# One operand of VectorE's weighing and of the edge sort's marks is read from PSUM instead of SBUF, in a four-layer graph network on one core

## The chip, the cores and the metric

The kernel runs on one core of one Trainium2 chip. The metric is the device time of one execution in microseconds (us), here the median of three runs. Matrix work is TensorE's (PE in the profile), elementwise work VectorE's (DVE) and ScalarE's (ACT), indirect DMAs are issued by GpSimd (POOL), plain ones by SyncE (SP).

## The reference

A graph of 6250 nodes with 256 features and 106250 edges, already sorted by destination, goes through four layers. Each is followed by a residual and a layer norm.

```python
src, dst = edge_index                       # 106250 edges, sorted by dst
# layer 0 (GIN)
agg = segment_sum(x[src], dst);   out = relu(bn(relu(bn(((1+eps)*x + agg) @ W1)) @ W2 + x))
# layer 1 (attention over edges, 8 heads of 32)
sim = einsum('hed,hed->eh', q[dst], k[src]) * scale
p = exp(sim - segment_max(sim, dst)[dst]);  attn = p / segment_sum(p, dst)[dst]
agg = segment_sum(attn * v[src], dst)
# layer 2 (edge attributes summed by SOURCE node, plus degree and centrality terms)
sum3d = segment_sum(edge_attr @ W_sum, src)
# layer 3 (gated; mean of neighbours in both directions, then a GRU cell)
```

## The kernel before

The kernel is a chain of eleven stages with a barrier after each (`end_stage`). The nodes are cut into NW = 49 blocks of 128. The edges are cut into NC = 832 chunks of 128, and the work over edges is STEPS = 880 steps: a chunk that spans two blocks of nodes is taken once for each. U = 16 steps make an iteration, QUAD = 4 steps are handled by one VectorE instruction, HALF = 8 steps is the depth of the rings of one-hot matrices, OCT = 8 chunks go together where edge rows are sorted.

A segment sum is a matrix product: VectorE compares the destinations of a chunk with `iota_row` (`compare`, L195, four chunks in one instruction of 128x512 elements) and TensorE multiplies this one-hot matrix by the chunk's rows into the PSUM bank of the block. ScalarE copies a finished bank out and clears it (`take_banks`, L186 and L188).

Three stages matter here.

**The first gather** (`first_gather`) sums the rows of x over the incoming edges. GpSimd issues 832 indirect gathers (L578), four at a time, into a ring of 16 slots; before each four it waits for `s_used`, which SyncE passes on when TensorE has used the slots. TensorE runs 880 products (L612). Beside this, `bin_positions` works out where each edge goes when edges are sorted by source: it *counts* edges by block of source nodes in a first half and *ranks* them in a second. Each takes 104 instructions called `mark` (L472): 8 chunks of source blocks, compared with the numbers 0 to 48 from `iota_row`, which gives a bf16 one-hot of 128x392. In the second half `widen` (L480), `place` (L488 and L491) and TensorE's `rank` (L435, L437) follow each mark. The mark's PSUM neighbours are `bp_counts` (two banks) and `bp_spread` (two banks).

**The weighted sums** (`weighted_sums`) compute the sum of attn * v and the sum of attn per block. SyncE loads the gathered v rows in quads of 512 KB (L1473) into `ring`, 16 slots; from the fifth quad on it waits until the quad that lay there is weighed. VectorE handles each quad with three instructions: `hot` compares (L195) and copies the 8 attention weights per edge beside the row (L1514); `weigh` (L1524) multiplies 128x1024 elements of `ring` by the weights, which are read from `k.sims` and repeated 32 times:

```python
weight = k.sims[:, s * HEADS:(s + QUAD) * HEADS].rearrange("p (s h) -> p s h", h=HEADS)
dve.tensor_tensor(weighted[...], ring[...], weight.unsqueeze(3).to_broadcast([P, QUAD, HEADS, HD]), ALU.mult)
```

`weighted` and `onehot` hold 8 steps, so VectorE may be two quads ahead of TensorE's products (L1504). In the same stage the edge attributes are sorted by source: GpSimd scatters 568 chunks of edge rows (71 octs of 8, L1280) from the two buffers of `staging` to `bin_rows` in DRAM. SyncE loads an oct (520 KB, L1265) after every third quad (WS_PACE = 12), in the same queue, and first waits until the scatters of the oct two before have landed. So a period of the stage is one oct of scatters on GpSimd, and on SyncE one load of an oct and three loads of quads, which stand behind it in order.

**The edge scores** (`edge_scores`) and the **last gathers** (`last_gathers`) are not touched. They also have GpSimd issue an indirect DMA per chunk (L1166, L2083) beside VectorE, and are read for comparison. In the edge scores VectorE multiplies a query row in PSUM by a key row in SBUF (L1239).

The order of work on each engine is the order in the code. Semaphore waits are the only coupling.

## Time and profile before

| what | value |
|---|---|
| three runs | 7632.49, 7638.13, 7615.44 us |
| median | 7632.49 us |
| span of the profiled execution, first to last instruction | 7527.2 us |
| the profiled execution's own time | not among the figures at hand; the span lies 105.3 us under the median of the runs |
| busy: PE, DVE, ACT, POOL | 5373.7, 3160.7, 545.2, 4732.4 us |
| mean granted TensorE clock | 0.750 of full speed |
| first gather | about 58 to 1360 us of the span |
| weighted sums | about 3400 to 4276 us of the span |

The busy times are sums over stages with different limits, so a change in a stage has to be read from the rows of that stage. "Idle before" is the time for which the engine did nothing before the instructions of a group, and the names behind it say what ended it.

### The profile page before, as it was taken

The page shows a single profiled execution, that of the slowest core. Times are in us where ns is not written, and L with a number is a line of the kernel's source. Part 1 is how long each engine was busy: PE and PEld are TensorE (multiplying, and loading weights), DVE is VectorE, ACT ScalarE, POOL GpSimd, SP SyncE. Part 2 cuts the span into 40 slices and gives each one's busy share as a digit, 9 for nine tenths or more (in the row PEclk, how much of TensorE's full clock was granted, in tenths as well). Part 3 has the DMA queues.
Part 4 walks back from the last instruction along what each step waited for, and adds up shares of the span by engine and source line. Part 5 has one row for each costly group of instructions (what it writes and reads, how often), then busy time and mean ns, then how long its engine had stood idle before and what let it go on. Part 6 is the DMA issues. An engine that isn't in the chain of part 4 may idle for free. (4 is left out here: it accounts for less than half of the span.)

```text
span 7527.2 us, 81611 instructions
## 1 busy us (share of the span) xinstructions
PE 5373.7 (71%) x17807; PEld 3065.0 (41%) x17807; DVE 3160.7 (42%) x6956; ACT 545.2 (7%) x1542; POOL 4732.4 (63%) x4778
## 2 busy tenths in 40 slices
PE   5666777638765556636566687788888888888887
PEld 2333333525332223324444575433433344444444
DVE  2222444528655556674444567511111123333317
ACT  0000000324000000010000001100000000000004
POOL 5666665664666666677677404766666666666665
PEclk8777777969767777767778899865555588888869
DMA  4444433331688888846667675433333333333445
GB/s 137 133 134 130 124 123 121 128 100 66 214 256 256 265 262 268 266 134 210 210 217 226 205 191 148 126 89 89 90 89 87 89 111 119 119 119 119 123 101 191
DMA packets 693161, 1164.20 MB, mean 155 GB/s; under 512 B 104128, under 2 KB 490285, under 8 KB 692614
## 3 DMA queue, kind: packets, MB, share of 16 engines
q0 software_dynamic: 224288, 633.55, 28.9%
q1 hardware_dynamic: 468344, 525.21, 21.9%
q8 instruction: 217, 3.56, 0.2%
q14 instruction: 202, 1.65, 0.1%
q10 hardware_dynamic: 110, 0.23, 0.0%
HBM read 870.83 MB, written 287.77 MB: 154 GB/s over the span
## 5 line engine op out<-in xcount | busy, mean ns | idle before, releaser
L2126 PE MATMUL l_sums<-big 128*128 (+1 forms) x3520 | 1701.9, 578 | 349.1 <-issue 135.1
L195 DVE TENSOR_TENSOR big<-iota_row,dst_tab 128x512 f32<-128x512 f32 x660 | 458.4, 695 | 2171.3 <-PE l_sums L2126 712.1
L1280 POOL DMA_INDIRECT bin_rows<-staging,place_tab x832 | 979.6, 1177 | 337.4 <-issue 249.1
L1166 POOL DMA_INDIRECT big<-kv_rows,idx_tab x880 | 832.0, 945 | 503.0 <-issue 241.1
L578 POOL DMA_INDIRECT big<-in_x,big x832 | 826.6, 994 | 483.6 <-SPq L148 237.7
L2083 POOL DMA_INDIRECT big<-x_rows,place_tab x880 | 882.3, 1003 | 394.9 <-issue 241.7
L2083 POOL DMA_INDIRECT big<-x_rows,idx_tab x832 | 817.2, 982 | 426.7 <-issue 226.6
L1220 PE MATMUL es_q<-big 128*128 x1760 | 720.9, 536 | 450.3 <-issue 343.3
L2126 PEld LDWEIGHTS l_sums<-big 128*128 128x128 f32 x3520 | 765.2, 259 | 502.0 <-issue 473.7
L612 PE MATMUL l_sums<-big 128*128 x1760 | 723.0, 543 | 331.9 <-issue 235.8
L1504 PE MATMUL ws_sums<-big 128*128 128x264 f32 x1760 | 546.1, 474 | 321.2 <-DVE big L1524 170.9
L1220 PEld LDWEIGHTS es_q<-big 128*128 128x128 f32 x1760 | 380.6, 252 | 747.7 <-issue 714.1
L612 PEld LDWEIGHTS l_sums<-big 128*128 128x128 f32 x1760 | 393.8, 255 | 623.9 <-issue 587.7
L1239 DVE TENSOR_TENSOR big<-es_q,big 128x256 f32<-128x256 f32 x880 | 370.8, 423 | 547.4 <-remote 274.3
L1504 PEld LDWEIGHTS ws_sums<-big 128*128 128x128 f32 x1760 | 400.6, 236 | 467.7 <-issue 384.9
L178 PEld LDWEIGHTS l_spare<-ones 128*1 128x1 bf16 x1760 | 139.7, 79 | 906.7 <-issue 906.7
L1244 DVE TENSOR_REDUCE sims<-big 128x8 f32<-128x256 f32 x880 | 356.1, 410 | 0.0
L1524 DVE TENSOR_TENSOR big<-big,sims 128x1024 f32<-128x1024 f32 x220 | 268.7, 1221 | 180.5 <-DMA big<-v_edge 173.6
L195 DVE TENSOR_TENSOR big<-iota_row,bin_tab 128x512 f32<-128x512 f32 x220 | 151.8, 692 | 440.4 <-PE l_sums L2126 263.8
L178 PE MATMUL l_spare<-ones 128*1 128x1 bf16 x1760 | 289.3, 164 | 3.4 <-issue 3.4
L1581 PE MATMUL as_sums<-sims 128*128 128x129 f32 x1760 | 249.8, 298 | 56.2 <-DVE sims L195 54.9
L1581 PEld LDWEIGHTS as_sums<-sims 128*128 128x128 f32 x1760 | 232.8, 189 | 74.5 <-issue 67.9
(297 smaller groups left out, 5187.4 us busy)
## 6 DMA issues: line engine op xcount, KB each, us to landing
v_edge<-big SPq DMA_DIRECT2D x880, 128.0 KB
big<-v_edge SPq DMA_DIRECT2D x220, 512.0 KB
bin_rows<-big SPq DMA_DIRECT2D x110, 520.0 KB
sims<-bin_rows SPq DMA_DIRECT2D x110, 520.0 KB
staging<-in_edges SPq DMA_DIRECT2D x104, 520.0 KB
gate_rows<-big SPq DMA_DIRECT2D x49, 512.0 KB
big<-gate_rows SPq DMA_DIRECT2D x49, 512.0 KB
big<-kv_rows,idx_tab POOLq DMA_INDIRECT x880
```

The costliest lines, as they stand in the source:

```text
L178: pe.matmul(spare, ones[:, 0:1], ones[:, 0:1], start=True, stop=True)
L195: return dve.tensor_tensor(out, rows, columns.unsqueeze(2).to_broadcast([P, QUAD, P]), ALU.is_equal)
L578: pool.indirect_dma_start(ring[:, u, 0:D], None, table, bass.IndirectOffsetOnAxis(ap=k.by_chunk[:, c:c + 1], axis=0)).then_inc(s_row[u], 16)
L612: pe.matmul(sums[:, bank_of(node[u], width)], onehot[:, u % HALF, :], flat[:, bass.ds(slot_of(s, node[u], D + 1), width)], start=False, st ...
L1166: pool.indirect_dma_start(ring[:, u, :], None, k.kv_rows, bass.IndirectOffsetOnAxis(ap=k.idx[:, s:s + 1], axis=0)).then_inc(s_row[u], 16)
L1220: pe.matmul(qps[u % 4][:, 0:D], onehot[:, u % HALF, :], query[:, bass.ds(block_at[u] * D, D)], start=True, stop=True).then_inc(s_q, 1)
L1239: dve.tensor_tensor(prod[:, u % 2, :], qps[u % 4][:, 0:D], ring[:, u, 0:D], ALU.mult).then_inc(s_prod, 1)
L1280: pool.indirect_dma_start(k.bin_rows, bass.IndirectOffsetOnAxis(ap=k.place[:, c:c + 1], axis=0), k.staging[:, g % 2, j, :], None).then_inc ...
L1504: pe.matmul(sums[:, bank_of(node[s % U], AW)], onehot[:, s % HALF, :], weighted[:, s % HALF, :], start=False, stop=True, skip_group_check= ...
L1581: pe.matmul(sums[:, bank_of(node[s % U], EW)], onehot[:, s % U, :], ring[:, q % RING, r, 2:2 + EW], start=False, stop=True, skip_group_che ...
L2083: pool.indirect_dma_start(ring[:, u, :], None, k.x3_rows, bass.IndirectOffsetOnAxis(ap=column, axis=0)).then_inc(s_row[u], 16)
L2126: pe.matmul(sums[:, bank_of(node[u] + turn, D)], onehot[:, u % HALF, :], flat[:, bass.ds(at, D)], start=False, stop=True, skip_group_check ...
```

## The change

In the weighted sums two PSUM tiles `ws_side0` and `ws_side1` of 128x128 are added (the stage then uses six banks). Once per iteration of 16 steps VectorE copies the iteration's 128 weights from `k.sims` to one of them (`keep`, 55 copies of 128x128), an iteration ahead, and both `hot`'s small copy and `weigh` read the weights from there. In `bin_positions` VectorE copies the numbers 0 to 48 once for each of the two halves to an unused part of a PSUM bank that is not written in that half (`bp_spread0` while counting, `bp_counts` while ranking), and all marks read them from there.

```diff
@@ bin_positions
+    numbers = spread[0][:, OCT * NW:OCT * NW + NW], counts[:, 1, ROWS // 2:ROWS // 2 + NW]
...
         def mark(n, g):
 
             if g == 0:
-                dve.wait_ge(s_row, 2)
+                if n:
+                    dve.wait_ge(s_wins, 3)
+                else:
+                    dve.wait_ge(s_row, 2)
+                dve.tensor_copy(numbers[n], k.iota_row[:, 0:NW]).then_inc(s_number, 1)
+                dve.wait_ge(s_number, n + 1)
...
-            dve.tensor_tensor(hot[:, g % 2, :, :], k.iota_row[:, 0:NW].unsqueeze(1).to_broadcast([P, OCT, NW]),
+            dve.tensor_tensor(hot[:, g % 2, :, :], numbers[n].unsqueeze(1).to_broadcast([P, OCT, NW]),
                               bin_f[:, g * OCT:(g + 1) * OCT].unsqueeze(2).to_broadcast([P, OCT, NW]),
                               ALU.is_equal).then_inc(s_hot, 1)
@@ weighted_sums
+        side = [psum(nc, ctx, f"ws_side{i}", [P, U * HEADS]) for i in range(2)]
...
+            def weights(s):
+
+                at = s % U * HEADS
+                return side[s // U % 2][:, at:at + QUAD * HEADS].rearrange("p (s h) -> p s h", h=HEADS)
+
+            def keep(it):
+
+                if it >= 2:
+                    dve.wait_ge(s_weight, (it - 1) * U)
+                    dve.wait_ge(s_side, (it - 1) * U)
+                dve.tensor_copy(side[it % 2][:, :], k.sims[:, it * U * HEADS:(it + 1) * U * HEADS]).then_inc(s_kept, 1)
...
-                dve.tensor_scalar(weighted[:, s % HALF:s % HALF + QUAD, D:], k.sims[:, s * HEADS:(s + QUAD) * HEADS].rearrange(
-                    "p (s h) -> p s h", h=HEADS), 1.0, None, ALU.mult).then_inc(s_side, QUAD)
+                dve.wait_ge(s_kept, s // U + 1)
+                dve.tensor_scalar(weighted[:, s % HALF:s % HALF + QUAD, D:], weights(s), 1.0, None,
+                                  ALU.mult).then_inc(s_side, QUAD)
...
-                weight = k.sims[:, s * HEADS:(s + QUAD) * HEADS].rearrange("p (s h) -> p s h", h=HEADS)
+                weight = weights(s)
...
+            keep(0)
             for s in range(0, STEPS, QUAD):
+                if s % U == 0 and s + U < STEPS:
+                    keep(s // U + 1)
                 hot(s)
                 weigh(s)
```

VectorE's instructions at the start of the weighted sums, before (`big` holds `ring`, `weighted` and `onehot`):

```order
L1528 MEMSET big 1x512
L195 TENSOR_TENSOR big<-iota_row,dst_tab 128x512
L1514 TENSOR_SCALAR big<-sims 128x4x8
L1524 TENSOR_TENSOR big<-big,sims 128x4x256
L195 TENSOR_TENSOR big<-iota_row,dst_tab 128x512
L1514 TENSOR_SCALAR big<-sims 128x4x8
L1524 TENSOR_TENSOR big<-big,sims 128x4x256
```

And with the change:

```order
L1548 MEMSET big 1x512
L1526 COPY ws_side<-sims 128x128 x2
L195 TENSOR_TENSOR big<-iota_row,dst_tab 128x512
L1534 TENSOR_SCALAR big<-ws_side 128x4x8
L1544 TENSOR_TENSOR big<-big,ws_side 128x4x256
L195 TENSOR_TENSOR big<-iota_row,dst_tab 128x512
L1534 TENSOR_SCALAR big<-ws_side 128x4x8
L1544 TENSOR_TENSOR big<-big,ws_side 128x4x256
```

Nothing is reordered; a copy comes in ahead of every fourth quad, two ahead of the first. L1524 becomes L1544, and L1514 becomes L1534.

VectorE at the start of the ranking half in the first gather, with the change:

```order
L195 TENSOR_TENSOR big<-iota_row,dst_tab 128x512 x2
L469 COPY bp_counts<-iota_row 128x49
L478 TENSOR_TENSOR big<-bp_counts,sims 128x392
L486 TENSOR_TENSOR big<-ident,sims 49x392
L195 TENSOR_TENSOR big<-iota_row,dst_tab 128x512
L478 TENSOR_TENSOR big<-bp_counts,sims 128x392
L486 TENSOR_TENSOR big<-ident,sims 49x392
```

The mark, L472 before, is L478 now, and one copy stands ahead of the first. The widening (L480, now L486) still reads both operands from SBUF. The other engines' instructions are the same as before.

## Rows read from the trace of the kernel before

**Rows 1.** Groups of instructions by line in the weighted sums, 3400 to 4276 us.
```profile
line engine op names shapes xcount | busy us, mean ns | idle before us <-releasers
L1280 POOL DMA_INDIRECT bin_rows<-staging,place_tab x568 | 637.4, 1122 | 239.7 <-issue 184.9 <-DMA staging<-in_edges 39.0 <-POOLq L108 15.8
L1504 PE MATMUL ws_sums<-big 128*128 128x264 f32 x1760 | 546.1, 474 | 321.2 <-DVE big L1524 170.9 <-issue 149.0 <-ACT ws_sums L188 1.0
L1524 DVE TENSOR_TENSOR big<-big,sims 128x1024 f32<-128x1024 f32 x220 | 268.7, 1221 | 180.5 <-DMA big<-v_edge 173.6 <-remote 3.7 <-PE ws_sums L1504 2.5
L195 DVE TENSOR_TENSOR big<-iota_row,dst_tab 128x512 f32<-128x512 f32 x220 | 153.3, 697 | 266.2 <-PE ws_sums L1504 160.4 <-remote 78.3 <-issue 27.5
L1514 DVE TENSOR_SCALAR big<-sims 128x32 f32<-128x32 f32 x220 | 51.0, 232 | 0.0
```
**Rows 2.** Waits of SyncE's queue and of GpSimd there: total us, times, longest.
```profile
SPq L1265 <- DMA bin_rows<-staging,place_tab: 200.4, 21, 11.7
SPq L1473 <- DVE big L1524: 117.4, 53, 14.4
...
POOL bin_rows L1280 <- DMA staging<-in_edges: 39.0, 4, 12.8
```
**Rows 3.** The scatters of that stretch alone: min/median/max ns, first and last start.
```profile
L1280 POOL DMA_INDIRECT bin_rows<-staging,place_tab x568: 963/969/2033, 3400.3 to 4260.6; - x190
```
**Rows 4.** Timeline of one period: start, length in us, engine, line, [idle before].
```profile
3547.96 1.23 DVE L1524 TENSOR_TENSOR big<-big,sims 128x1024 f32<-128x1024 f32 x1 [4.48 <-DMA big<-v_edge]
3548.51 1.52 POOL L1280 DMA_INDIRECT bin_rows<-staging,place_tab  x1 [0.30 <-issue]
...
3552.16 0.97 POOL L1280 DMA_INDIRECT bin_rows<-staging,place_tab  x1 [0.30 <-issue]
3553.20 0.35 SPq L1265 DMA_DIRECT2D staging<-in_edges  x1
...
3553.59 1.56 SPq L1473 DMA_DIRECT2D big<-v_edge  x3
...
3561.37 0.69 DVE L195 TENSOR_TENSOR big<-iota_row,dst_tab 128x512 f32<-128x512 f32 x1 [0.95 <-remote]
3561.61 1.29 POOL L1280 DMA_INDIRECT bin_rows<-staging,place_tab  x1 [0.30 <-issue]
```
**Rows 5.** Edge scores: GpSimd's gathers, and VectorE's product that reads PSUM; min/median/max ns.
```profile
L1166 POOL DMA_INDIRECT big<-kv_rows,idx_tab x880: 940/946/1002, 1942.0 to 3260.8; - x176
...
L1239 DVE TENSOR_TENSOR big<-es_q,big x880: 412/425/426, 1946.0 to 3277.0; 128x256 f32<-128x256 f32 x176
```
**Rows 6.** Last gathers, first half: GpSimd's gathers twice, then VectorE's compares, 4800 to 6037 us.
```profile
L2083 POOL DMA_INDIRECT big<-x_rows,idx_tab x832: 940/946/1461, 4803.5 to 6036.2; - x167
...
L2083 POOL DMA_INDIRECT big<-x_rows,idx_tab x832 | 817.2, 982 | 426.7 <-issue 226.6 <-SPq L148 189.8 <-POOLq L108 10.3
...
L195 DVE TENSOR_TENSOR big<-iota_row,dst_tab 128x512 f32<-128x512 f32 x219 | 151.7, 693 | 1027.1 <-PE l_sums L2126 712.1 <-issue 191.1 <-remote 123.8
```
**Rows 7.** First gather: gathers twice, the mark, the widening, and the place's product that reads PSUM.
```profile
L578 POOL DMA_INDIRECT big<-in_x,big x832: 940/946/1656, 58.7 to 1351.6; - x167
...
L578 POOL DMA_INDIRECT big<-in_x,big x832 | 826.6, 994 | 483.6 <-SPq L148 237.7 <-issue 229.5 <-POOLq L108 16.4
...
L472 DVE TENSOR_TENSOR big<-iota_row,sims 128x392 bf16<-128x392 f32 x208 | 116.5, 560 | 0.0
...
L480 DVE TENSOR_TENSOR big<-ident,sims 49x392 f32<-49x392 f32 x104 | 57.7, 555 | 0.0
L488 DVE TENSOR_TENSOR big<-bp_spread,big 128x392 f32<-128x392 f32 x104 | 57.5, 553 | 0.0
```
**Rows 8.** Busy time and DMA in the 8 us behind a load of an oct, and in the 3 us after.
```profile
core 0: us, PE busy (x) PEld busy (x) DVE busy (x) ACT busy (x) POOL busy (x), PEclk, DMA share, GB/s
3553.00:3561.00 8.00, 4.83 (x18) 3.41 (x18) 3.94 (x6) 0.00 (x0) 6.17 (x7) 0.93 0.91 284
3561.00:3564.00 3.00, 3.00 (x8) 2.28 (x8) 1.91 (x3) 0.00 (x0) 2.39 (x3) 0.50 0.37 122
```
**Rows 9.** Timeline of a stall in the weighted sums.
```profile
3655.36 0.69 DVE L195 TENSOR_TENSOR big<-iota_row,dst_tab 128x512 f32<-128x512 f32 x1 [12.83 <-remote]
...
3657.70 0.51 SPq L1265 DMA_DIRECT2D staging<-in_edges  x1
...
3662.76 1.53 POOL L1280 DMA_INDIRECT bin_rows<-staging,place_tab  x1 [10.43 <-DMA staging<-in_edges]
```
**Rows 10.** A VectorE pass over 128x128 elements between PSUM and SBUF, in the softmax stage.
```profile
L1395 DVE TENSOR_SCALAR big<-sm_t 128x128 f32<-128x128 f32 x55 | 11.8, 288 | 3.2 <-PE sm_t L1362 2.7 <-issue 0.4
```

More of the change, by code:

```diff
@@ L387, in bin_positions @@
     spread = [psum(nc, ctx, f"bp_spread{i}", [P, 512]) for i in range(2)]
-    s_fill, s_filled, s_key, s_hot, s_counted, s_line, s_start, s_wins, s_spread, s_taken, s_row, s_wide = sems(
+    numbers = spread[0][:, OCT * NW:OCT * NW + NW], counts[:, 1, ROWS // 2:ROWS // 2 + NW]
+    s_fill, s_filled, s_key, s_hot, s_counted, s_line, s_start, s_wins, s_spread, s_taken, s_row, s_wide, s_number = sems(
         nc, k, *(f"bp_{n}" for n in ("fill", "filled", "key", "hot", "counted", "line", "start", "wins", "spread",
-                                     "taken", "row", "wide")))
+                                     "taken", "row", "wide", "number")))
     COUNT_AT, LINE_AT, PLACE_AT = 4, 424, 452
@@ L1460, in weighted_sums @@
         sums = psum(nc, ctx, "ws_sums", [P, BANKS * BANK])
-        s_zeros, s_hot, s_weight, s_side, s_sum, s_taken, s_free = sems(
-            nc, k, *(f"ws_{n}" for n in ("zeros", "hot", "weight", "side", "sum", "taken", "free")))
+        side = [psum(nc, ctx, f"ws_side{i}", [P, U * HEADS]) for i in range(2)]
+        s_zeros, s_hot, s_weight, s_side, s_sum, s_taken, s_free, s_kept = sems(
+            nc, k, *(f"ws_{n}" for n in ("zeros", "hot", "weight", "side", "sum", "taken", "free", "kept")))
         s_v = sems(nc, k, *(f"ws_v{q}" for q in range(U // 2)))
```

## The prediction

> **What bounds the kernel now.** The change touches two of eleven stages, so I read those, and two others for comparison. In the weighted sums the groups by line come first [rows 1]. VectorE is busy for 268.7 + 153.3 + 51.0 = 473 of 876 us and TensorE for 546.1; both wait for a large part. GpSimd hardly does. Its 568 scatters take 637.4 us, and of its 239.7 us idle 184.9 lie between one scatter and the next without any wait (0.33 us each), 15.8 at the start; only 39.0 us are a wait, for the load of an oct. 637.4 + 184.9 + 39.0 + 15.8 = 877.1: the whole stage. SyncE confirms it: it stood 200.4 us until scatters had landed before it could load the next oct [rows 2], and the loads of v stand behind that load in its queue, so VectorE's wait for v (173.6 us) and TensorE's for VectorE (170.9 us) are made there. GpSimd's scatters pace this stage.
>
> Then the length of a scatter. Its median is 969 ns, its least 963 and its most 2033 [rows 3], the mean 1122. The timeline shows what lengthens it [rows 4]: a scatter that starts during L1524 takes 1.52 us and ends at 3550.03, 0.84 us after L1524 (3549.19); one with VectorE quiet takes 0.97 us. The same under the compare L195: 1.29 us, end at 3562.90, 0.84 us after L195 (3562.06). So GpSimd comes soon after its start to a point that it can't pass while VectorE runs one of these two, and both read two operands from SBUF. The control is the edge scores: there 880 products L1239 read one operand from PSUM, and of 880 gathers none took over 1002 ns against a median of 946 [rows 5].
>
> **The weighing.** Scatters above their median: 568 x (1122 - 969) ns = 87 us. This is due to L1524 and L195, and the change takes only L1524 out of it. What L195 alone costs I take from the last gathers, where nearly all that VectorE does is L195: 832 x (982 - 946) ns = 30 us for 219 of them [rows 6]. The weighted sums have 220, and gathers there are spaced alike, so 30 us remain. It may be less, since a scatter held by L1524 today can't be held by the L195 behind it; then what is left is today's share of L195. Term: -(87 - 30) = **-57 us**. Bounds: -87 if nothing holds a scatter, and 0 if a PSUM operand does not free it. I take -57 because the rows 5 and 6 show both halves of it at hundreds of instructions.
>
> Can the rest of the stage follow? A period (an oct of scatters, three quads) lasts 877 / 71 = 12.4 us now and would last 8 x (0.969 + 30/568 + 0.326) = 10.8 us, without the waits. VectorE's work in a period is 3 x (1.22 + 0.70 + 0.23) = 6.5 us, TensorE's 546.1 / 73 = 7.5 us. DMA: after a load of an oct is issued the engines are 0.91 busy for 8 us and then 0.37 [rows 8], so a burst of 2.1 MB needs some 8 of the 10.8 us. All three fit.
>
> In four places the period was not GpSimd's: VectorE stood for up to 12.83 us for something that the profile puts down as "remote", the loads in SyncE's queue came late, and GpSimd then waited, once 10.43 us [rows 9], in sum 39.0 us in four waits [rows 2]. I see no wait in the code for it, and leave it as it is. But a shorter period leaves less in hand when it happens: about 1 us more in each of the four waits, **+4 us**.
>
> **What the weighing costs.** L1544 has as many elements as L1524. A PSUM operand does not change the pace: L488 with one takes 553 ns, L480 of as many elements per partition, all in SBUF, 555 [rows 7]. The 55 copies into PSUM I take at the 288 ns of a 128x128 pass out of PSUM [rows 10]: 16 us of VectorE. Each follows a wait for VectorE's own last instruction, some 0.1 us. What hides them is VectorE's idle time, 180.5 + 266.2 us in the stage; without it they would be 16 to 22 us on the path. Their operand in SBUF is one, so by rows 5 they hold no scatter; if they did, 16 us of cover against 473 would add 2 us. **0 us**, at most +2.
>
> **The marks.** In the first gather the gathers lie 832 x (994 - 946) ns = 40 us above their median [rows 7]. L195's part is 30 us again; 10 are left for 208 marks and 104 widenings, which keep both operands in SBUF and will, in the second half, catch some gathers that the mark before them holds now. So 7 to 10 us of GpSimd's time go. But GpSimd is not alone on the path: it waited 237.7 us for slots that TensorE had not yet used [rows 7], and where such a wait follows, a shorter gather only lengthens the wait. Half counts: **-4 us**, between 0 and -10. Two copies of 128x49 are nothing.
>
> **Sum.** -57 + 4 - 4 = -57 us. The profiled execution's own time is not shown; its span of 7527.2 us goes to 7470, and what lies around it I leave alone: 7632.5 - 57 = **7576 us** against the median, -0.7%.
>
> **Rivals.**
> *The hold does not depend on where the second operand lies.* Then nothing moves but 20 us of hidden copies: 7632 us. Against it stand 880 gathers beside L1239; for it only that L1239 is shorter (0.42 us), which would make holds shorter, not absent. Chance 0.04. The Trainium skill has a rule on this side: "SBUF — State Buffer", section "Who interferes with whom", says that a VectorE instruction with two SBUF inputs stands in the way of a GpSimd instruction that reads SBUF, not of one that only writes it, and infers that generating a DMA's descriptors needs only the write side, so that `tensor_tensor` does not delay it. By that, today's scatters would not be held and the change would be worth 0; the trace of rows 3, 4 and 6 disagrees, at least for indirect DMAs.
>
> *The stalls take it back.* The bursts of loads follow each other at 10.8 us with 8 us of DMA work, so a late burst runs into the next, SyncE's queue stands, and GpSimd waits more often. Each stall as in rows 9 costs about 10 us; if their number doubles, 39 us come back: -57 + 39 = -18, 7615 us. From about three more on the gain is under 0.3%. For it: four stalls exist. Against: most periods today end with the DMA engines at 0.37. Chance 0.11.
>
> *VectorE becomes the bound,* because the weights in PSUM, repeated 32 times and read beside TensorE's writes to other banks, come slowly. Place: L1544. Its three per period fit until 3 x (0.93 + w) = 10.8, w = 2.7 us; from w = 3.2 us on the stage is slower than today. At 3.5 us, 73 x 3 x 4.43 = 970 us against 876: about 7722 us. Against it: L488 reads PSUM beside TensorE's products at the pace of L480 [rows 7], and the 880 of L1239 never took over 426 ns [rows 5]. Chance 0.03.
>
> *More is saved:* L195's share stays at what it is today, and the stalls shrink with luck: 57 becomes 72 to 87, 7545 to 7560 us. Chance 0.12, faster too.
>
> **How the numbers follow.** The forecast, -35 to -72 us, has 0.70. About 0.3% (23 us) is what a measurement of this kernel can tell from no change. Faster: 0.70 + 0.12 and the part of the stalls that leaves over 23 us (0.03), 0.85. Same: 0.04 + 0.07, 0.11. Slower: 0.03 and 0.01 for stalls beyond that, 0.04. The range runs from 7547, nearly the lower bound of GpSimd's share, to 7615, where the stalls have doubled.
>
> **What would show it.** L1280 in the weighted sums: mean from 1122 to about 1022 ns, busy 580 us, and no scatter that ends 0.84 us after L1544. L1544 at 1.22 us; L1526 at 0.2 to 0.3. The stage from 876 to about 824 us. L578's mean from 994 to about 985. L1166 and L2083 as before. I am wrong if L1280's mean stays above 1080 (the hold), if it falls and GpSimd's wait for `staging` grows by as much (stalls), or if L1544 passes 2 us.

## The result and the profile after

The changed kernel took **7708.1 us** (median of four runs, 7674.6 to 7719.8) against 7624.0 us (7597.0 to 7638.1, four runs) for the kernel before: ratio 1.0104, 95% interval 1.0074 to 1.0134. It is 1% slower. The forecast was 7576, 0.7% faster, and the range ended at 7615.

The profiled execution has a span of 7697.6 us. By stage, before and after: first gather 1307 and 1302 us, edge scores 1337 and 1383, weighted sums **876 and 978**, last gathers 2525 and 2554. Edge scores and last gathers have the same instructions in both kernels; in the other profiles they lie between 1323 and 1384 and between 2510 and 2560 us (the last comparison below apart), so their part of the difference is not the change's. Nor is all of the 170 us between the two spans: the execution profiled before (7527.2 us) was about 100 us shorter than the runs beside it. The comparison of `ws_only` with `marks_only` below, which stand side by side on one chip, is the cleaner one: stages of 960 and 875 us, kernels of 7607.3 and 7511.7.

The groups by line of the weighted sums in the changed kernel, which answer to [rows 1]:

```profile
line engine op names shapes xcount | busy us, mean ns | idle before us <-releasers
L1286 POOL DMA_INDIRECT bin_rows<-staging,place_tab x568 | 571.4, 1006 | 398.4 <-DMA staging<-in_edges 200.4 <-issue 182.2 <-POOLq L108 15.9
L1511 PE MATMUL ws_sums<-big 128*128 128x264 f32 x1760 | 548.3, 471 | 420.4 <-issue 210.3 <-DVE big L1544 206.0 <-ACT ws_sums L188 3.4
L1544 DVE TENSOR_TENSOR big<-big,ws_side 128x1024 f32<-128x1024 f32 x220 | 266.2, 1210 | 10.7 <-issue 5.4 <-DMA big<-v_edge 5.3
L195 DVE TENSOR_TENSOR big<-iota_row,dst_tab 128x512 f32<-128x512 f32 x220 | 152.5, 693 | 526.0 <-remote 327.8 <-PE ws_sums L1511 139.5 <-issue 57.6
...
L1526 DVE COPY ws_side<-sims 128x128 f32<-128x128 f32 x55 | 16.1, 294 | 1.8
```

The scatters did what was forecast and more: mean 1122 to 1006 ns, 637.4 to 571.4 us. But GpSimd's wait for its edge rows in `staging` went from 39.0 us in 4 waits [rows 2] to 200.4. VectorE no longer waits for v (173.6 to 5.3 us) but in front of the compare L195, 266.2 to 526.0 us, most of it "remote". The same in the waits of the stage:

```profile
SPq L1480 <- DVE big L1544: 418.3, 112, 19.2
SPq L1271 <- DMA bin_rows<-staging,place_tab: 28.9, 5, 9.0
...
POOL bin_rows L1286 <- DMA staging<-in_edges: 200.4, 20, 14.8
```

SyncE used to wait for scatters to land (200.4 us, now 28.9) and now waits for VectorE (117.4, now 418.3). The pace has passed from GpSimd to VectorE, which is busy for only 435 of 978 us. Its timeline (start, length, [idle before]) shows the form of the loss, the one of [rows 9]:

```profile
4106.54 0.69 DVE L195 TENSOR_TENSOR big<-iota_row,dst_tab 128x512 f32<-128x512 f32 x1 [13.29 <-issue]
4107.15 0.18 DVE L1534 TENSOR_SCALAR big<-ws_side 128x32 f32<-128x32 f32 x1
4107.26 1.21 DVE L1544 TENSOR_TENSOR big<-big,ws_side 128x1024 f32<-128x1024 f32 x1
4117.12 0.69 DVE L195 TENSOR_TENSOR big<-iota_row,dst_tab 128x512 f32<-128x512 f32 x1 [8.65 <-remote]
```

L195 waits for one thing, `s_sum`, TensorE's count of its products. From the trace's records of that semaphore, beside the ends of the products (counted from 0; the ends are modelled):

```
4090.33 product 571 ends   (the one that L195 of 4106.54 needs)
4096.93 product 575 ends   (the one that L195 of 4117.12 needs)
count +1 at 4095.14 4099.40 4102.93 4112.05 4115.55
count +1 at 4116.98 4117.02 4117.07 4117.11 4117.15 4117.19
```

One count has no record: the one that lets L195 go, whose wait ends at 4106.5. Counts come 3 to 6 us apart, where products 572 to 575 end 0.8 to 0.9 us apart; then six come within 0.21 us, quicker than TensorE makes products (two matmuls of 0.47 us each). So products had been done that were not yet counted: **the counts are late, not the products**. L195 of 4106.54 starts 16 us after the modelled end of the product that it needs. I measured for each compare how long after both (VectorE free, product ended) it starts. Sum of those over 1 us late, and number over 5 us: before 132 us and 9, after 453 us and 37.

It is TensorE's counts that are late. VectorE's own are on time in the same stage: of the 219 quads behind the first, none has its first product over 0.56 us after L1544 has ended and TensorE is free, and SyncE, when it waits for VectorE, issues the load of v 0.03 us after L1544. ScalarE, which waits for TensorE's counts too, starts up to 12.1 us after the last product that ended.

The records have gaps of their own. In the weighted sums 682 of TensorE's 881 counts have one, and 121 of VectorE's 220 weighings; in the kernel before it is 644 and 138, in `after_busy` and in the last comparison below all of them. In `before_deep` records are missing (703 of 881) and no compare is late, so a missing record alone makes no late count. Whether the capture of the profile has a part in the delay is open: no run here was timed without a span captured on its core.

On the product ends the Trainium skill ("Perfetto Trace Analysis", section "Tensor Engine Instruction (MATMUL, LD_WEIGHTS)") says that the profiler estimates them, and that the count is sent only when PSUM has acknowledged the write and has then to propagate. So an ending in the profile is not a count; the bursts are what tells late counts from slow products here.

While this stall lasts GpSimd scatters on at its full pace, until `staging` is empty (SyncE's next load stands behind the v loads, which stand behind VectorE):

```profile
4108.38 0.97 POOL L1286 DMA_INDIRECT bin_rows<-staging,place_tab  x1 [0.30 <-issue]
...
4112.20 0.97 POOL L1286 DMA_INDIRECT bin_rows<-staging,place_tab  x1 [0.30 <-issue]
4124.34 0.97 POOL L1286 DMA_INDIRECT bin_rows<-staging,place_tab  x1 [11.17 <-DMA staging<-in_edges]
```

The burst of counts comes at 4117, 3.8 us after the last scatter ended at 4113.2. All the stalls that end in a burst (three counts or more, each at most 0.08 us behind the other: 22 after, 5 before; one more comes behind the very last scatter) end in a pause of GpSimd, 1.3 to 4.8 us after it ran dry. This gives the **theory**: a stream of scatters without breaks delays TensorE's counts to VectorE; the change makes the stream denser. **Rivals**: something that the change adds (the PSUM reads, the copies, their waits); nothing following the products on TensorE; the number of counts; VectorE's short lead of two quads.

### The profile page after: what moved, and what is told of

It is laid out like the page before. It is cut to its first block and busy times, and to the rows that moved or that the text cites. A ratio compares the mean times of both kernels' runs of the same rounds, so it can differ in the third digit from the quotient of the medians.

```text
span 7697.6 us, 81941 instructions
## 1 busy us (share of the span) xinstructions
PE 5365.1 (70%) x17807; PEld 3045.6 (40%) x17807; DVE 3167.0 (41%) x7013; ACT 545.2 (7%) x1542; POOL 4658.5 (61%) x4778
## 5 line engine op out<-in xcount | busy, mean ns | idle before, releaser
L2149 PE MATMUL l_sums<-big 128*128 (+1 forms) x3520 | 1681.4, 571 | 398.8 <-issue 154.0
L195 DVE TENSOR_TENSOR big<-iota_row,dst_tab 128x512 f32<-128x512 f32 x660 | 457.7, 694 | 2452.4 <-PE l_sums L2149 742.8
L1286 POOL DMA_INDIRECT bin_rows<-staging,place_tab x832 | 913.4, 1098 | 490.2 <-issue 246.6
L2106 POOL DMA_INDIRECT big<-x_rows,place_tab x880 | 885.2, 1006 | 397.7 <-issue 238.3
L584 POOL DMA_INDIRECT big<-in_x,big x832 | 818.1, 983 | 484.8 <-SPq L148 236.5
L178 PEld LDWEIGHTS l_spare<-ones 128*1 128x1 bf16 x1760 | 139.2, 79 | 892.8 <-issue 892.8
L195 DVE TENSOR_TENSOR big<-iota_row,bin_tab 128x512 f32<-128x512 f32 x220 | 151.7, 691 | 441.9 <-PE l_sums L2149 274.6
L178 PE MATMUL l_spare<-ones 128*1 128x1 bf16 x1760 | 288.8, 164 | 1.0 <-issue 1.0
L1544 DVE TENSOR_TENSOR big<-big,ws_side 128x1024 f32<-128x1024 f32 x220 | 266.2, 1210 | 10.7 <-issue 5.4
L2062 PE MATMUL gp_g<-sims,big 128*128 128x512 f32 x392 | 237.5, 690 | 40.2 <-DVE big L2022 35.7
```

Of the source, the lines that this page charges most:

```text
L178: pe.matmul(spare, ones[:, 0:1], ones[:, 0:1], start=True, stop=True)
L195: return dve.tensor_tensor(out, rows, columns.unsqueeze(2).to_broadcast([P, QUAD, P]), ALU.is_equal)
L584: pool.indirect_dma_start(ring[:, u, 0:D], None, table, bass.IndirectOffsetOnAxis(ap=k.by_chunk[:, c:c + 1], axis=0)).then_inc(s_row[u], 16)
L1286: pool.indirect_dma_start(k.bin_rows, bass.IndirectOffsetOnAxis(ap=k.place[:, c:c + 1], axis=0), k.staging[:, g % 2, j, :], None).then_inc ...
L2106: pool.indirect_dma_start(ring[:, u, :], None, k.x3_rows, bass.IndirectOffsetOnAxis(ap=column, axis=0)).then_inc(s_row[u], 16)
L2149: pe.matmul(sums[:, bank_of(node[u] + turn, D)], onehot[:, u % HALF, :], flat[:, bass.ds(at, D)], start=False, stop=True, skip_group_check ...
```

## The experiments

Each comparison has its own runs of the kernel before beside it, on the same chip, and ratios are to those. Stage times are the weighted sums in the profile; "late" is the sum and number defined above.

### Which part of the change

`ws_only` is the change in `weighted_sums` alone, `marks_only` that in `bin_positions` alone. `copies_only` keeps the 55 copies into PSUM and VectorE's wait for them, but reads the weights from SBUF:

```diff
-                at = s % U * HEADS
-                return side[s // U % 2][:, at:at + QUAD * HEADS].rearrange("p (s h) -> p s h", h=HEADS)
+                return k.sims[:, s * HEADS:(s + QUAD) * HEADS].rearrange("p (s h) -> p s h", h=HEADS)
```

Expected of `ws_only`:

> The change in the weighted sums alone; the marks read SBUF as before. In the profile of the changed kernel the weighted sums took 968 us between the first and last product against 867, the first gather 1288 against 1292. Theory 1 (late counts: the loss is in the weighted sums, where VectorE waits in front of L195 for TensorE's count of products while TensorE has nothing to do): all of the loss stays, about 7700 us, and the scatters' mean near 1006 ns with GpSimd's wait for staging near 200 us. Rival (the marks, or code that is displaced, cost the time in other stages): near 7625 us.

Expected of `marks_only`:

> The marks alone read PSUM; the weighted sums are those of before. Theory 1: 7620 us, the gathers' mean in the first gather near 983 ns against 994, the stage shorter by 4 to 8 us, the weighted sums near 870 us with GpSimd's wait for staging near 40. Rival (displaced code makes the stalls): weighted sums well above 900 us here too.

Expected of `copies_only`:

> The changed kernel with its copies of the weights into PSUM and its waits, but both reads of the weights go back to SBUF, so that L1524's hold on GpSimd is there again; the marks stay in PSUM. Theory 2 (VectorE's hold was a break in GpSimd's stream of scatters, and without breaks TensorE's counts reach VectorE late): the stage comes back to 870 to 890 us, waits in front of L195 as 'remote' to about 90 us, the ratio to the kernel before 0.997 to 1.002. Rival (the added copies and waits disturb VectorE): the stage stays near 960 us, ratio 1.012.

Measured: `ws_only` 1.0119 [1.0088, 1.0150], stage 960 us, late 419 us. `marks_only` 0.9987 [0.9965, 1.0010], stage 875. `copies_only` 1.0019 [0.9994, 1.0043], stage 875, scatters 1141 ns, late 138 us. The loss is the weighted sums', and there not the copies' or the waits': it comes with the PSUM operand of L1544, that is with what this does to the scatters, or with the PSUM reads themselves.

### What TensorE does behind a product, and how often it counts

```diff
                 pe.matmul(sums[...], onehot[...], weighted[...], ...).then_inc(s_sum, 1)
+                push(pe, k, spare[:, 0:1])
```

is `after_push` and `before_push`: a 1x1 product (L178) behind each product, as the gather stages have it. `after_quad_count` lets TensorE count by 4 on the last product of a quad, a quarter of the counts.

Expected of `after_push`:

> The changed kernel, with a product of one column by one (L178, the helper push that the last gathers have) behind every product of the weighted sums. Theory 1 (a finished product is counted late while nothing follows it on TensorE): the counts come in time, VectorE's 328 us of waiting as 'remote' in front of L195 go, GpSimd's wait for staging falls from 200 us to under 40, the stage takes 800 to 830 us and the kernel about 7560 to 7590. Rival (VectorE's wait comes of its own added copies and waits, or of its instruction supply): no change but 880 small products, 7700 us or a little more.

Expected of `before_push`:

> The kernel before with the same small product behind every product of the weighted sums. Theory 1: the four stalls of 39 us in all go, the scatters' mean stays near 1122 ns, the stage 830 to 850 us, the kernel 7590 to 7610. Rival: 7625 us or a little more.

Expected of `after_quad_count`:

> The changed kernel, but TensorE counts its products four at a time, on the last of each quad, instead of one by one. Theory 2 with a backlog of counts as its core: a fourth of the counts makes a backlog shorter, GpSimd's wait for staging falls from 190 us to under 60, the stage takes 810 to 850 us, ratio 0.985 to 0.995, faster than both. Rival (the products themselves are late, not their counts): 960 us as before, ratio 1.012.

Measured: `after_push` 1.0140 [1.0103, 1.0176], stage 948, late 256 us with up to 24.7 in one compare, GpSimd's wait for staging 150.7; `before_push` 1.0097 [1.0067, 1.0127], stage 947, late 147 us. Neither forecast came true: something that follows at once does not end the stalls. The smaller sum after the change is no cure, since VectorE now waits longer for the products themselves (279.5 us in place of 139.5; in the kernel before 319.9 in place of 160.4, where the stage loses 71 us).

`after_quad_count` 1.0107 [1.0080, 1.0135], stage 985, GpSimd's wait for staging 208.8 us, late 467 us: as the change. I had forecast a gain, and by the expectation this outcome speaks for slow products; the bursts above speak against those. What it does rule out is the number of counts. The Trainium skill ("TensorE: Matmul & The Clock Gate", section "The cost: per-tile semaphore tail") prices a count at some 26 ns and advises one on the last product. Here a quarter of the counts gave nothing, and delays of 10 us are hundreds of times that price.

### With no scatters, and with breaks between them

`after_no_scatter` leaves out the loads and scatters of edge rows in the weighted sums, but for the first two octs (the edge attributes are partly not sorted). `after_pause` puts a memset of 128x384 elements and a wait for it behind every fourth scatter:

```diff
-                spread_oct(pool, k, g)
+                for first in range(0, OCT, QUAD):
+                    spread_part(pool, k, g, first, QUAD)
+                    pool.memset(scratch, 0.0).then_inc(s_pause, 1)
+                    pool.wait_ge(s_pause, (g - EARLY_OCTS) * 2 + first // QUAD + 1)
```

`after_lumped` has nearly as many (140 for 142), four in a row after every second oct.

Expected of `after_no_scatter`:

> The changed kernel without the scatters of edge rows in the weighted sums but for the first two octs, and without the loads that feed them, so the edge attributes of layer 2 are partly left out. Theory 2: without GpSimd's stream no count is late; VectorE's waits in front of L195 as 'remote' vanish (under 20 us), the stage is bound by products and loads: 220 quads at 2.1 to 2.6 us, 460 to 570 us. Rival (the loads of v or the PSUM reads delay the counts): late counts of over 100 us remain.

Expected of `after_pause`:

> The changed kernel, but GpSimd makes a break after every fourth scatter: a memset of 128x384 of a scratch area and a wait for it, estimated at 0.5 to 0.8 us from the 0.20 us of a 128x128 memset, so about as much in all (142 breaks) as the holds took away. Theory 2: with the breaks the late counts go back to the level of before, GpSimd's wait for staging falls from about 190 us to 40 to 80, the stage takes 870 to 900 us although GpSimd has more to do, ratio near 1.00. Rival (reading the weights from PSUM beside TensorE's writes delays the products' counts): 960 to 1000 us, since GpSimd's breaks only add.

Expected of `after_lumped`:

> The changed kernel with the same GpSimd pauses as the kernel with a pause after every fourth scatter (142 memsets of 0.44 us with a wait behind each), but four of them one behind the other after every second oct, so that 16 scatters follow each other without a break and then comes one break of some 3 us. If what restores the time is that GpSimd's stream has breaks often, long counts come back: the stage is well above the 902 us of the kernel with the spread pauses, 930 to 980. If it is only GpSimd's pace, or the total time without scatters, the stage is about 902 us, ratio within 0.3% of 1.

Measured: without scatters (one execution) the stage takes 498 us, with the same products, v loads and PSUM reads, and late is 6 us in two compares. They are the control within the run: the 16 scatters that are left end at 3462.6 us, the two late compares start at 3457.2 (1.1 us late) and 3464.3 (5.2), and in the 470 us after them none is late. So neither the PSUM reads nor the v loads delay the counts. With pauses (`after_pause`): 0.9995 [0.9969, 1.0020], stage 902, just above the 870 to 900 expected, GpSimd's wait for staging 58.8 us. `after_lumped` 0.9988 [0.9965, 1.0012], stage 870:

```profile
L1286 POOL DMA_INDIRECT bin_rows<-staging,place_tab x568 | 573.9, 1010 | 215.8 <-issue 175.5 <-DMA staging<-in_edges 18.3 <-POOLq L108 15.8
...
L195 DVE TENSOR_TENSOR big<-iota_row,dst_tab 128x512 f32<-128x512 f32 x220 | 153.2, 697 | 389.9 <-PE ws_sums L1518 183.8 <-remote 183.0 <-issue 22.6
...
L1499 POOL MEMSET big<- 128x384 f32 x140 | 59.2, 423 | 6.1
```

Giving back to GpSimd the 65 us (59.2 + 6.1) that the change had taken from it takes GpSimd's wait from 200.4 to 18.3 us. I had expected breaks far apart to be worse than frequent ones (930 to 980 us if frequency mattered). They were not: four memsets, some 2 us, after every second oct are enough. The lateness fell less than the wait (298 us and 28 over 5 us, none over 11.1): a stall that ends before GpSimd runs dry does not cost GpSimd, which paces the stage, anything.

### Still denser, and a deeper ring

`after_no_hold` lets the compare read its row of numbers from PSUM too, so that nothing holds a scatter:

```diff
+        numbers = psum(nc, ctx, "ws_numbers", [P, P])
...
-                compare(dve, k, onehot[:, s % HALF:s % HALF + QUAD, :], None, k.dst[:, s:s + QUAD]).then_inc(s_hot, QUAD)
...
+                compare(dve, k, onehot[:, s % HALF:s % HALF + QUAD, :], numbers[:, :].unsqueeze(1).to_broadcast([P, QUAD, P]), k.dst[:, s:s + QUAD]).then_inc(s_hot, QUAD)
```

`after_deep` and `before_deep` make the rings `weighted` and `onehot` 16 steps deep (`DEEP = 2 * HALF`), so that VectorE may be four quads ahead.

Expected of `after_no_hold`:

> The changed kernel, with the numbers that the compare of the weighted sums takes read from a PSUM tile as well, so that no VectorE operation over many elements reads two operands from SBUF in that stage. Both theories: no scatter is held any more, mean from 1006 to about 970 ns, another 20 us of GpSimd's time gone (568 x 36 ns). The theory of late counts (the products' counts reach VectorE late for as long as GpSimd's scatters follow each other closely): the scatters leave still less room, so the stalls in front of the compare stay or grow, GpSimd waits 200 us or more for staging, and the stage takes 977 to 1000 us; ratio 1.010 or more. The rival (the time was lost to something that belongs to the weighing reading PSUM beside an operation with two operands in SBUF, or to the holds that are left): the stage takes less than with the change, 950 us or below.

Expected of `after_deep`:

> The changed kernel with rings of 16 steps in place of 8 for the weighed rows and for the rows of ones, so that VectorE may be four quads ahead of TensorE's counted products in place of two. If counts only arrive late (TensorE itself works on), eight products more of slack, some 3 to 5 us, absorb most stalls of 5 us and part of those of 10 to 18: GpSimd's wait for staging falls from 200 to below 80 us, the stage to 830 to 880 us, and the kernel is as fast as before or up to 0.6% faster. If TensorE's products themselves are slow, a deeper ring fills as well and nothing is gained: the stage stays at 960 us or more, ratio 1.010.

Expected of `before_deep`:

> The kernel before with the same rings of 16 steps, as the measure of what the rings alone bring: it had stalls too, 39 us of GpSimd's waiting for staging. If late counts are what the ring absorbs, the stage falls from 876 to 850 to 865 us and the ratio is 0.997 to 0.999, so the changed kernel with deep rings beats it by the rest of the holds removed (20 to 50 us). If nothing is absorbed: 876 us, ratio 1.

Measured: `after_no_hold` 1.0170 [1.0117, 1.0223], the slowest of the complete kernels, stage 1016 us:

```profile
L1286 POOL DMA_INDIRECT bin_rows<-staging,place_tab x568 | 551.6, 971 | 450.8 <-DMA staging<-in_edges 255.9 <-issue 179.1 <-POOLq L108 15.8
...
L195 DVE TENSOR_TENSOR big<-ws_numbers,dst_tab 128x512 f32<-128x512 f32 x220 | 151.7, 690 | 570.8 <-remote 383.0 <-PE ws_sums L1512 142.9 <-issue 44.1
```

Its longest scatter takes 982 ns. Twenty more us taken from GpSimd cost 38 us more of the stage; that is the theory's side, and the stage is longer than the 977 to 1000 us expected. The two ratios come from different comparisons, and their intervals touch.

The deep rings I had wrong. `after_deep` is at 1.0113 [1.0061, 1.0165], stage 953, late 479 us with up to 19.8: a lead of eight more steps absorbs nothing. That fell on the side that I had given to slow products. But the bursts are there, and the finding above explains it otherwise: a stall lasts until GpSimd stops, so a longer lead only moves the moment at which VectorE runs dry. Its bursts agree: most hold 11 to 15 counts, where the change has 4 to 6, and come 2.1 to 5.5 us after GpSimd ran dry. `before_deep` is at 1.0001 [0.9978, 1.0024], stage 867, with not one compare late, and its row shows why:

```profile
L1280 POOL DMA_INDIRECT bin_rows<-staging,place_tab x568 | 673.6, 1186 | 200.3 <-issue 184.7 <-POOLq L108 15.7
```

With VectorE never waiting for counts more scatters are held, and the mean is 1186 ns. Nor does the deep ring hide late counts here: among the records there is no burst. GpSimd did not wait for staging at all, yet the kernel is as fast as before: what stalls had cost (39.0 us), holds cost now (673.6 - 637.4 = 36 us). In the order of the scatter's mean length, the sums late of all kernels so far without added pauses: 1186 ns 0 us, 1141 ns 138, 1136 ns 103, 1122 ns 132, 1103 ns 147, 1049 ns 256, 1007 ns 419, 1006 ns 453, 998 ns 467, 992 ns 479, 971 ns 491. These come from several chips, one execution each. Part of this order could run the other way, since a VectorE that stands holds no scatter; in `after_no_hold` the length is set by the edit alone.

### What it is in the scatters

`after_busy` puts a memset of 128x1152 and a wait in the place of each scatter (the edge attributes are partly not written); `after_half_rows` cuts each scatter to its first 64 rows (the others are not written). Each ran once.

Expected of `after_busy`:

> The changed kernel with a GpSimd memset of about 1.2 us and a wait for it in the place of each of the 568 scatters of the weighted sums (the edge attributes are therefore partly not written); the loads of the octs stay and wait for the memsets. If a busy GpSimd is what delays TensorE's counts, there are waits of the compare of over 5 us as in the changed kernel and the stage is above 900 us. If it is the descriptors or their transfers, there are none: the compare's waits marked remote are below 30 us and the stage follows GpSimd at about 71 x 8 x 1.33 = 755 us, or whatever TensorE and VectorE need beyond that, up to 800 us.

Expected of `after_half_rows`:

> The changed kernel with every scatter of the weighted sums cut to the first 64 of its 128 rows (the edge attributes of the others are not written). If it is the number of descriptors, or of the small transfers, that crowds out TensorE's counts, half of them ends the stalls: compare's waits marked remote from 328 to below 100 us, GpSimd's wait for staging below 50 us. If it is the scatter instructions as such, whatever their size, the stalls stay or, where the scatters become shorter, grow: remote 328 us or more.

Measured, `after_busy`: stage 655 us, no compare late by over 0.5 us:

```profile
L1501 POOL MEMSET big<- 128x1152 f32 x568 | 601.2, 1058 | 48.0 <-POOLq L108 15.2
...
L195 DVE TENSOR_TENSOR big<-iota_row,dst_tab 128x512 f32<-128x512 f32 x220 | 151.4, 688 | 91.4 <-PE ws_sums L1517 90.6 <-issue 0.4
```

The stage is 100 us shorter than I had expected: a memset took 1.06 us where I had set 1.2, and 0.08 us lie between two. `after_half_rows`: stage **1057 us**, more than any other:

```profile
L1496 POOL DMA_INDIRECT bin_rows<-staging,place_tab x568 | 518.8, 913 | 520.4 <-DMA staging<-in_edges 270.6 <-issue 233.8 <-POOLq L108 15.9
...
L195 DVE TENSOR_TENSOR big<-iota_row,dst_tab 128x512 f32<-128x512 f32 x220 | 152.2, 692 | 614.8 <-remote 478.2 <-PE ws_sums L1514 118.2 <-issue 17.1
```

A busy GpSimd delays nothing. Indirect DMAs do, and not in proportion to their rows: half the rows, at a shorter distance, delay more (532 us, 44 over 5 us). That what counts is how closely one indirect DMA follows the other fits all these runs, but no run changes that distance alone: in `after_half_rows` it is 1.2 us from start to start in place of 1.3, and the rows are halved with it.

### Stopping GpSimd when VectorE is late

If a stall lasts because the scatters go on, ending them early should end it. `after_gate` makes GpSimd wait, before every fourth scatter, for what VectorE has weighed (in undisturbed periods that stands at step 12n - 4 when oct n begins and at 12n in its middle, so the wait is for one quad less than that, and not for two less as the expectation has it); `after_gate_loose` has 16 for 8, and `before_gate` is the kernel before with the tight wait.

```diff
             for g in range(EARLY_OCTS, OCTS):
-                spread_oct(pool, k, g)
+                for first in range(0, OCT, QUAD):
+                    weighed = (g - EARLY_OCTS) * WS_PACE + first - 8
+                    if weighed > 0:
+                        pool.wait_ge(s_weight, weighed)
+                    spread_part(pool, k, g, first, QUAD)
```

Expected of `after_gate`:

> The changed kernel; before every fourth scatter GpSimd also waits until VectorE has weighed all but two quads of what stood weighed at that point in the undisturbed periods of the kernel before (steps 12n - 8 before oct n, 12n - 4 before its second half). In undisturbed periods this wait is over before it begins. If a stall lasts because the scatters go on during it, GpSimd now stops within some 5 us of its start, the stalls end after about 5 us in place of 10 to 18, the longest wait of the compare falls below 10 us, and the stage takes 840 to 880 us: the kernel about as fast as before or up to 0.5% faster. If a stall lasts for a reason of its own, the pauses only add to it: the stage is 980 us or more, ratio 1.011 or above.

Expected of `after_gate_loose`:

> The same with the wait two quads looser (12n - 16 and 12n - 12). By the theory that going on makes the stall last, it lies between the tight wait and the changed kernel: the longest waits of the compare 10 to 14 us, the stage 870 to 930 us. By the rival no difference from the changed kernel beyond 10 us (977 us).

Measured: `after_gate` **0.9965** [0.9947, 0.9982], stage 893; `after_gate_loose` 0.9998 [0.9979, 1.0016], stage 906. The first is faster than the kernel before and, by its ratio, than the changed one. Of the waits of `after_gate`:

```profile
DVE big L195 <- remote: 203.5, 29, 12.2
...
POOL bin_rows L1286 <- DVE big L1548: 117.6, 31, 6.8
```

Longest wait of the compare: 17.7 us with the change, 17.8 with the loose gate, where I had set 10 to 14, and 12.2 with the tight one, where I had set below 10. Late are 453, 358 and 285 us. The stage lies in the order expected, 978, 906, 893, though the last is above its upper end (880). Of the 25 bursts with the tight gate 24 fall in a pause of GpSimd, 1.2 to 3.1 us after its last scatter.

Last, a gate before every second scatter (`after_gate_fine`), and the gate in the kernel before.

Expected of `after_gate_fine`:

> The changed kernel with GpSimd's wait for VectorE's progress before every second scatter (steps 12n - 8, 12n - 8, 12n - 4 and 12n weighed before scatters 1, 3, 5 and 7 of oct n) in place of every fourth. If going on during a stall is what prolongs it, the compare's longest wait falls from 12.2 to below 10 us, its waits marked remote below 203.5 us, and the stage from 893 to 850 to 885 us; ratio to the kernel before 0.993 to 0.996. If the tighter wait only holds GpSimd up, the stage is 900 us or more and the ratio 0.998 or above.

Expected of `before_gate`:

> The kernel before with the wait before every fourth scatter. It had four stalls with 39 us of GpSimd's waiting; if the gate shortens them, the stage falls from 876 to 855 to 870 us and the ratio is 0.997 to 0.999. If the gate were the whole of the gain of the changed kernel with it, this kernel would be as fast as that one, ratio 0.996 or below.

These two ran with a kernel before that took 6651.9 us (15 runs, 6646 to 6669), on a chip where it had taken 7512.9 (19 runs, 7488 to 7565) in an earlier comparison. What had changed there is not shown by any run. TensorE's granted clock does not explain it: in the edge scores, at 1337 and 1110 us, it was 0.71 and 0.72 (in the first gather, at 1307 and 1100 us, 0.71 and 0.79). Within the comparison: `after_gate_fine` **0.9868** [0.9851, 0.9885], 6567.3 us; `before_gate` 1.0000 [0.9991, 1.0009]. Neither has a single late count in the weighted sums (largest 0.5 us):

```profile
L1286 POOL DMA_INDIRECT bin_rows<-staging,place_tab x568 | 573.5, 1010 | 197.2 <-issue 173.4 <-POOLq L108 10.3 <-DVE big L1548 9.9
...
L1548 DVE TENSOR_TENSOR big<-big,ws_side 128x1024 f32<-128x1024 f32 x220 | 267.5, 1216 | 208.2 <-DMA big<-v_edge 204.5 <-PE ws_sums L1515 3.1
L195 DVE TENSOR_TENSOR big<-iota_row,dst_tab 128x512 f32<-128x512 f32 x220 | 152.2, 692 | 124.0 <-PE ws_sums L1515 123.1
```

and of `before_gate`:

```profile
L1280 POOL DMA_INDIRECT bin_rows<-staging,place_tab x568 | 653.2, 1150 | 196.4 <-issue 178.6 <-POOLq L108 11.7 <-DMA staging<-in_edges 5.8
```

So the fine gate's effect on stalls is not shown: there were none, and it waited 9.9 us in all. What the pair shows is better: where counts are on time, the change (with its gate) is worth 79.7 us of scatters (653.2 - 573.5), the stage goes from 849 to 778 us and the first gather from 1100 to 1084, the kernel from 6652 to 6567. The gate alone gives nothing (1.0000). The changed kernel without a gate was not run under these conditions.

The two conditions side by side say where late counts cost. Stages of the kernel before, and of `before_gate` in the last comparison, in us: first gather 1307 and 1100, the stage behind it 414 and 325, edge scores 1337 and 1110, last gathers 2525 and 2208, all with indirect DMAs beside the compute; projection 160 and 160, attribute sums 314 and 314, close of attention 211 and 210, with none. A gather lasts the same (L1166 948 ns in `before_deep`, 946 in `before_gate`). What goes is waiting. GpSimd's wait for slots of the first gather, 237.7 us in [rows 7], is in `before_gate`

```profile
POOL big L578 <- SPq L148: 8.2, 27, 0.3
```

and of VectorE's waits in the edge scores this one of the kernel before is gone:

```profile
DVE big L1239 <- remote: 274.3, 83, 7.0
```

## Why the prediction was wrong, step by step

**The bound** was read rightly: GpSimd's scatters paced the stage, 637.4 of 877 us.

**The weighing, -57 us**: right in GpSimd's time, a little low. The scatters' excess over their median fell from 87 to 568 x (1006 - 969) ns = 21 us (30 forecast), so GpSimd saved 66 us. A PSUM operand frees the scatters from L1544; with the compare's also in PSUM the longest scatter is 982 ns (`after_no_hold`). So the hold follows the second SBUF operand. The Trainium skill ("SBUF — State Buffer", section "Who interferes with whom") infers that `tensor_tensor` leaves descriptor generation alone. The trace disagrees as far as indirect DMAs go: of the 568 scatters of before 186 were held.

**What the weighing costs, 0 us**: right. L1544 takes 1210 ns, the copies 294 ns each, hidden; `copies_only` lies within 0.3% of 1.

**The marks, -4 us**: L578, now L584, went from 826.6 to 818.1 us of GpSimd's time, the mean from 994 to 983 ns. In the kernel's time `marks_only` (0.9987) can't be told from 0. Right for this condition. It was GpSimd's wait of 237.7 us for slots that hid the rest: where that wait was 8.2 us, the gathers fell from 832.4 to 816.6 us and the stage by 16 us, more than the bound of 10.

**The stalls, +4 us: this step failed.** "But a shorter period leaves less in hand when it happens: about 1 us more in each of the four waits." Measured: 20 waits and 200.4 us in place of 4 and 39.0, +161 us against the 66 saved; the stage's +101 is near the difference of the two (95). I took the number of stalls as given and only their cover as shorter. But the stalls were not independent of the change: the dense stream makes them, and holds had been spacing it out. The holds had been a brake: by the trace of before, L1524 held 132 scatters for 71.5 us in all, and `after_lumped`, which gives GpSimd 65 us of breaks, brings its wait down to 18.3 us. The row was there: [rows 9] shows L195 waiting 12.83 us, marked remote, and of it I wrote "I see no wait in the code for it". That was false: L195 stands behind `dve.wait_ge(s_sum, s + QUAD - HALF + 1)`, the wait for TensorE's counts, with a lead of two quads. I left the cause open and yet priced its growth. Why TensorE's counts come late beside the scatters is still open.

**The rivals.** "The stalls take it back" was the right one by name, and by the sign that I gave for it: L1280's mean falls and GpSimd's wait for staging grows by as much. Its mechanism was wrong, bursts of loads that run into each other: `after_busy` has the same loads in 655 us, and nothing was late there. And its size was too small, with 39 us for a doubling: five times the waits came. It had 0.11, and only 0.01 of it on the slower side, since I let the number grow at most a few times. A stall of unknown cause in the very stage that is made denser should have had far more on that side. The other rivals did not come: the hold does depend on the operand, L1544 was never slow.

## What to carry to other kernels

Before a saving on the pacing engine is booked, look for waits on another engine's count ("remote", at 10 us and more) that are far longer than that engine's work, and ask whether they come with the pacing engine's density; if so, a faster stream can bring more of them, and their number is no constant. Beside a stream of indirect DMAs a consumer of TensorE's counts can be over 10 us late. A deeper ring did not help here (1.0113). GpSimd waiting on the consumer's progress every few DMAs did: it cost nothing where all was on time (1.0000) and let this change keep part of its gain (0.9965). The 0.9868 was measured where no count was late and the gate waited 9.9 us in all, so as far as the runs tell it is the change's gain and not the gate's. A contention that slows a stream may be what keeps the rest in step: where it is removed, a brake of your own may be needed in its place.

## What the runs showed of the hardware

- A stream of indirect DMAs on GpSimd can delay TensorE's semaphore counts, at VectorE by up to 24.7 us (`after_push`; 17.7 with the change). They arrive 3 to 6 us apart (the stall shown) and then in a burst 0.04 us apart, 1.3 to 4.8 us after the stream has stopped. VectorE's counts to TensorE and SyncE are on time beside it (at most 0.56 us). Memsets of 1.06 us in the scatters' place do not do it (`after_busy`), and 64 rows delay no less than 128 (532 us in `after_half_rows`). By which path the two meet is open.
- In the stages with late counts the profile's own records of counts have gaps (682 of 881 of TensorE's, 121 of 220 of VectorE's weighings); without late counts they were complete in `after_busy`, `after_gate_fine` and `before_gate`, and not in `before_deep`.
- It takes a condition of the chip as well: in one comparison of six no count was late and the kernel before took 6652 us in place of 7513 to 7652. What brings it about stays open.
- A GpSimd scatter is held while VectorE's `tensor_tensor` reads two operands from SBUF and ends 0.84 us after it [rows 4]; so 186 of 568 before, within 0.01 us. With one of them in PSUM it is not: 568 scatters of at most 982 ns (`after_no_hold`).
